# Third cross attention: GpSimd splits rows one tile at a time, and the output projection moves among the last two units

## The reference

```
xn = layer_norm(x_context, g1, b1)                  # 8 x 1601 x 256
ln_lat = layer_norm(latents, g2, b2)                # 8 x 64 x 256
q = ln_lat @ Wq                                     # 16 heads of 64
k, v = split(concatenate([xn, ln_lat]) @ Wkv)       # 1665 keys
weight = softmax(where(mask, q k^T / 8, -max))
out = (weight @ v) @ Wout                           # 1024 -> 256
x = x + out
```

## Time and profile before

| | before |
|---|---|
| median of 3 runs | 2664.39 us |
| the profiled execution, device time | 2679.92 us |
| its span | 2677.9 us |
| TensorE busy | 2377.3 us (89%) |
| VectorE busy | 1717.3 us (64%) |
| ScalarE busy | 1180.1 us (44%) |
| GpSimd busy | 892.6 us (33%) |
| mean granted TensorE clock | 0.956 |
| first and last instruction of the changed layer, about | 973 and 1679 us |

### The profile page before, as it was taken

The page is one execution under the profiler, slowest core; times in us unless marked ns, Lnnn a source line. Parts: engine busy times, 40 slices in busy tenths (PEclk is TensorE's granted clock), DMA queues, the critical chain, the costliest instruction groups (busy, mean ns, idle before and its releaser), DMA issues. The chain is left out here.

```text
span 2677.9 us, 44545 instructions
## 1 busy us (share of the span) xinstructions
PE 2377.3 (89%) x17457; PEld 1500.8 (56%) x17457; DVE 1717.3 (64%) x3309; ACT 1180.1 (44%) x1964; POOL 892.6 (33%) x543
## 2 busy tenths in 40 slices
PE   6866779999998879999999998689889999997898
PEld 4744446666663445556555565345546666665555
DVE  4986455555538586888888853754675665555577
ACT  2316134444443214555555553544445555553244
POOL 5610042224204312211222200068643454341286
PEclk8987889999998989999999999899999999999999
DMA  3200453323204025667765663033323233120132
GB/s 109 68 1 1 134 134 89 99 72 81 73 20 159 1 74 137 129 127 140 146 140 117 116 116 65 32 95 101 102 62 81 64 80 87 38 62 21 49 95 67
DMA packets 358464, 226.42 MB, mean 85 GB/s; under 512 B 289785, under 2 KB 326482, under 8 KB 358258
## 3 DMA queue, kind: packets, MB, share of 16 engines
q1 hardware_dynamic: 355186, 215.20, 33.3%
q0 software_dynamic: 3072, 8.39, 1.1%
HBM read 114.87 MB, written 0.52 MB: 43 GB/s over the span
## 5 line engine op out<-in xcount | busy, mean ns | idle before, releaser
L98 PE MATMUL PS<-hot 128*128 128x512 f16 x519 | 159.8, 451 | 97.1 <-DVE l0a_g L1053 18.3
L3891 PE MATMUL PS<-l2x_rows,l2x_pth 128*128 128x512 f16 x832 | 202.9, 383 | 17.1 <-DVE l2x_mean L4086 17.1
L3804 POOL TENSOR_TENSOR l2x_rows<-l2x_rows,l2x_one 128x1024 f16<-128x1024 f32 (+1 forms) x32 | 61.6, 1930 | 416.1 <-DVE l2x_rows L1405 416.1
L3562 DVE CUSTOM_DVE_ANT_0 l1x_junk<-PS,l1x_bias 128x1024 bf16<-128x1024 f32 (+1 forms) x128 | 123.3, 991 | 98.4 <-PE PS L3227 97.5
L4079 DVE TENSOR_TENSOR l2x_pl<-l2x_sc,l2x_ph 128x1664 f16<-128x1664 f32 x64 | 151.9, 2374 | 40.4 <-ACT l2x_ph L3960 37.8
L98 PEld LDWEIGHTS PS<-hot 128*128 128x128 f16 x519 | 53.2, 111 | 181.9 <-issue 50.7
L3562 DVE CUSTOM_DVE_ANT_0 l3x_junk<-PS,l3x_bias 128x1024 bf16<-128x1024 f32 (+1 forms) x128 | 123.6, 991 | 44.5 <-PE PS L3227 43.3
L4064 DVE CUSTOM_DVE_ANT_0 l2x_sc<-PS,l2x_bias 128x1665 f32<-128x1665 f32 x64 | 120.9, 1889 | 37.9 <-issue 37.0
L3978 ACT ACTIVATE l2x_meanT<-PS 128x256 f32<-128x256 f32 x64 | 24.5, 383 | 271.0 <-PE PS L3868 271.0
L3433 ACT ACTIVATE l3x_pT<-PS 128x512 f32<-128x512 f32 x144 | 84.6, 594 | 120.3 <-PE PS L3273 117.9
L3860 PE MATMUL PS<-l2x_kh,l2x_qth 128*128 128x512 f16 (+1 forms) x512 | 132.9, 341 | 3.8 <-DMA l2x_kl<-l2x_rows 3.8
(11 more groups left out here) (845 smaller groups left out, 6309.0 us busy)
## 6 DMA issues: line engine op xcount, KB each, us to landing
l2f_unit<-in_L_ffn_units_dram SPq DMA_DIRECT2D x36, 384.0 KB, 3.1
l3f_unit<-in_L_ffn_units_dram SPq DMA_DIRECT2D x34, 384.0 KB, 3.0
l1x_kst<-l1x_kh SPq DMA_DIRECT2D x128, 100.1 KB, 2.2
l3x_kst<-l3x_kh SPq DMA_DIRECT2D x128, 100.1 KB, 2.2
l2x_rows<-in_ctx_dram SPq DMA_DIRECT2D x8, 1536.0 KB
l1x_ctx<-in_ctx_t_dram SPq DMA_DIRECT2D x7, 1601.0 KB, 7.5
l3x_ctx<-in_ctx_t_dram SPq DMA_DIRECT2D x7, 1601.0 KB, 7.1
l1x_kst<-l1x_kl SPq DMA_DIRECT2D x64, 100.1 KB, 2.2
```

The lines of the kernel that those rows point to most:

```text
L98: self.nc.tensor.matmul(self.PS[:, bank, :], self.hot[:, 0:P], self.hot[:], start=True, stop=True)
L3562: v.tensor_tensor_reduce(junk[:, slot(it), 0:n], slot_banks(it)[:, 0:n], bias[:, 0 if normed else b % 2, at:at + n], 1.0, LOWEST, ALU.add, ...
L3804: nc.gpsimd.tensor_tensor(high, of, one[0:p, 0:n].unsqueeze(2).unsqueeze(3).to_broadcast([p, n, NC, P]), ALU.mult).then_inc(rows_high, 1)
L3891: nc.tensor.matmul(PS[:, ACC, :], pth[:, u % 2, m, :], rows2[:, b % 2, :, :, m, :], start=(m == 0), stop=False)
```

## The change

Two edits, both in `layer_2_xattn`.

1. GpSimd's `split_high` and `split_low` of batches 1 to 7 issue one operation for each row tile (128 x 256) instead of one for each part (128 x 1024 for four tiles). Only the last operation of a part raises the semaphore. Batch 0 stays as it was.
2. The output projection is cut by token tile and moved. `project_heads(t, heads)` does token tile t for a range of head pairs: tile 0 before the sums of unit 62, tile 1 before those of unit 63, tile 2 after unit 63, tile 3 with its first seven head pairs after the last mean's transposes, and its last head pair at the end. Tiles 0 and 1 go to bank 4, tile 2 to bank 6, tile 3 to bank 0. VectorE adds tiles 0 and 1 before the last mean, and tiles 2 and 3 one by one after it.

```diff
+    OUT_AT = [(PREP[0], 0), (PREP[0], D), (PREP[1], 0), (0, 0)]
...
+                def pieces(b, n):
+                    return [slice(i, i + 1) for i in range(n)] if b else [slice(0, n)]
+
                 def split_high(b, j):
                     n, p, of, high, _ = part_of(b, j)
                     pool.wait_ge(rows_made, NP_ * b + j + 1)
-                    nc.gpsimd.tensor_tensor(high, of, one[0:p, 0:n].unsqueeze(2).unsqueeze(3).to_broadcast([p, n, NC, P]), ALU.mult).then_inc(rows_high, 1)
+                    for at in pieces(b, n):
+                        i = at.stop - at.start
+                        last = nc.gpsimd.tensor_tensor(high[:, at], of[:, at],
+                                                       one[0:p, at].unsqueeze(2).unsqueeze(3).to_broadcast([p, i, NC, P]), ALU.mult)
+                    last.then_inc(rows_high, 1)
 
                 def split_low(b, j):
                     n, p, of, high, low = part_of(b, j)
                     pool.wait_ge(rows_high, NP_ * b + j + 1)
-                    nc.gpsimd.tensor_tensor(low, of, high, ALU.subtract).then_inc(rows_low, 1)
+                    for at in pieces(b, n):
+                        last = nc.gpsimd.tensor_tensor(low[:, at], of[:, at], high[:, at], ALU.subtract)
+                    last.then_inc(rows_low, 1)
...
+                def project_heads(t, heads):
+                    last_unit = (2 * t + 1) * R + heads[-1]
+                    pe.wait_ge(post_read, 2 * (last_unit + 1))
+                    bank, at = OUT_AT[t]
+                    for r in heads:
+                        last = nc.tensor.matmul(PS[:, bank, at:at + D], oT[:, r, t * P:(t + 1) * P],
+                                                wo[:, r, :], start=(r == 0), stop=(r == R - 1))
+                    if r == R - 1:
+                        last.then_inc(put_out, 1)
+
                 def unit(b, r):
                     u = b * R + r
                     if u + 2 < U:
                         scores(u + 2)
                     for group, of in fills(b, r):
                         prepare(group, of)
+                    if u == U - 2:
+                        pe.wait_ge(prep_read, len(made_as))
+                    if u + 2 >= U:
+                        project_heads(u + 2 - U, range(R))
                     pe.wait_ge(high_turned, 16 * (u + 1))
                     pe.wait_ge(sums_copied, u)
...
+                project_heads(2, range(R))
                 turn_means(U - 1)
+                pe.wait_ge(scored, U)
+                project_heads(3, range(R - 1))
                 project(U - 1)
-                pe.wait_ge(post_read, 2 * U)
-                st.end(project_tokens(k, two_banks(k, 0), [oT[:, r, :] for r in range(R)],
-                                      [wo[:, r, :] for r in range(R)]), "projected")
+                project_heads(3, range(R - 1, R))
...
+                dve.wait_ge(put_out, 2)
+                first_pair = k.X[:, 0:2, :].rearrange("p t d -> p (t d)")
+                link(v.tensor_tensor(first_pair, first_pair, PS[:, PREP[0], :], ALU.add))
                 make_means(U - 1)
-                st.wait(dve, "projected")
-                st.end(add_to_latents(k, 0), "added")
+                for t in range(2, NT):
+                    dve.wait_ge(put_out, t + 1)
+                    last = v.tensor_tensor(k.X[:, t, :], k.X[:, t, :], PS[:, OUT_AT[t][0], 0:D], ALU.add)
+                    if t == 2:
+                        link(last)
+                st.end(last, "added")
```

More of the change, by code:

```diff
@@ L3665, in ready @@
         return 1 + max(made_as[b, g] for g in groups)
-    st = Stages(k.sem("l2x_stage"), ["lat", "lat_psum", "lat_first", "lat_rest", "projected", "added"])
+    st = Stages(k.sem("l2x_stage"), ["lat", "lat_psum", "lat_first", "lat_rest", "added"])
     paced, tokens_high, tokens_low = k.sem("l2x_paced"), k.sem("l2x_tokens_high"), k.sem("l2x_tokens_low")
@@ L3680, in layer_2_xattn @@
     post_made, post_read = k.sem("l2x_post_made"), k.sem("l2x_post_read")
+    put_out = k.sem("l2x_put_out")
     with ExitStack() as c_:
```

## The result

The changed kernel takes 2639.26 us (median of four runs, 2637.24 to 2640.17), the kernel before 2662.72 us in four runs (2660.50 to 2664.89). The ratio is 0.9908, with a 95% interval of 0.989 to 0.9925: 0.9% faster.

A forecast was written before the change was run, and what follows sets the result against it. TensorE was taken to bound the kernel, idle in the layer's middle only for VectorE's mean. Splits -9.0 and tail -9.9 make -18.9 us: 2664.39 to 2645.5 us, with an 8-in-10 range of 2640 to 2660.

The forecast's parts named there:

- TensorE sets the pace: From 1040 to 1640 us TensorE bounds the layer, idle only for VectorE's mean: 14 waits, 12.2 us.
- `pl` gets in behind the first piece, at 2.3 us.: VectorE's `pl` beside GpSimd's splits: near 2.3 us in 18 places instead of 3.5 to 3.6, within TensorE's 0.57 us slack.
- The rival of four high pieces: Beside the splits, `pl` waits for all four high pieces: +7 us in the middle, 2661.5 us in all; chance 0.14.
- the one of all eight: Beside the splits, `pl` waits for all eight pieces of a part: +53 us, 2707 us in all; chance 0.06.
- The lean on L1597: VectorE gets in between queued GpSimd operations, as row L1597 did, though L123 stood 6.76 us through several.
- The first wait goes to 0, the second to 0.3, the 0.88 stays, the 0.50 is open; -9.0.: TensorE's waits for the mean in six batches: 1.15 us to 0, 0.66 to 0.3; the splits' term, -9.0 us.
- 12.2 us is all that any change of GpSimd's work can give.: Upper bound on the splits' gain in this layer: TensorE's summed idle waits for the mean, 12.2 us.
- The tail, -9.9.: Layer's end, moved output projection: 7.1 us of idle time filled and shorter addition, 2.8 us of clock; -9.9 us.
- The basis, 2664.39 us.: Starting time of the whole kernel before, the runs' median, from which the forecast's terms were subtracted.
- the pieces give back half: Low pieces hold `shift` and the scalings, so waits return next unit: splits give 2.5 us, 2652 in all; chance 0.20.
- The tail does not shrink: Layer's end: VectorE's addition delays the last mean or the clock falls; worth 3 us, inside the range, no separate chance.

The follow-up runs named there:

- e1: The kernel before with only the one-tile GpSimd splits of batches 1 to 7, old output projection; 2650.79 us, ratio 0.9957 to the kernel before.
- e7: The changed kernel with whole-part splits that, in batches 1 to 7, wait for the unit's `pl` to end; ratio 0.9905 to the kernel before.
- e9: The changed kernel with batch 0's splits also issued one tile to an operation; ratio 0.9908 to the kernel before.
- e4: The changed kernel with `split_high` issued whole again and only the low split tile by tile; ratio 0.9952 to the kernel before.
- e2: The changed kernel with the old whole-part splits, so only the moved output projection is new; 2652.41 us, ratio 0.9962 to the kernel before.
- e8: The changed kernel with batch 0's splits waiting until VectorE has written the normalised latents; ratio 0.9884 to the kernel before.

## Why the prediction was right in kind and short in size

Step by step, as it was put:

- **"TensorE sets the pace"; it stands idle "for one reason only", VectorE's mean.** Right in what counts, though the list that was read for it has a second entry, 1.2 us for ScalarE's `l2x_qb`, which no edit here touches. Taking the waits for the mean away gives the time, in e1 and e7 alike, and GpSimd's 26 us of more work (892.6 to 918.4 busy) cost nothing.
- **"`pl` gets in behind the first piece, at 2.3 us."** Right, but only at the first part of each of the six batches (2.33), six of the 18 places where 2.3 us was foretold; at the other twelve `pl` took 1.87, for the reason below. The slack of 0.57 us covered it. The rival of four high pieces and the one of all eight are refuted by that row. The lean on L1597 was right for high pieces; in e9 the low ones did what L123's row had shown. The Trainium skill's rule ("SBUF — State Buffer", section "Who interferes with whom": issue order decides who blocks) agrees with `pl` at 2.33, at 1.87 when it was issued 0.09 us ahead, and with the high pieces; by the same rule the L4161 of e9, issued 0.47 us ahead of the first low piece, would have got in behind at most the piece that ran, and it stood 8.95 us.
- **"The first wait goes to 0, the second to 0.3, the 0.88 stays, the 0.50 is open; -9.0."** This is the step that failed, by size: the mechanism held, and the term of -9.0 us measured -12.6, the shrinking of the middle. Two parts are measured. *The second wait went to 0, not 0.3* (6 x 0.3 = 1.8 us): the working had `shift` and the scaling held by the low pieces, about 1 us together and the next `pl` as late as before. `shift` was held by nothing (0.15 us), the scalings by 0.61 us, and just this hold put `pl` ahead of GpSimd (1.87 us). That a stage can be late enough to win the next one was not thought of. *A wait costs more than the idle time that the profile shows.* The idle time of TensorE in the middle fell from 13.39 to 2.34 us, by 11.05, and the middle by 12.58, over twelve waits: 0.13 us a wait beside its idle time, 1.5 us in all. e4 against the changed kernel gives the same (12.44 of time, 10.94 of idle time), and e1 against e2 (12.07 and 10.60), all at a granted clock of 1.00. The two that stayed fell by 0.15 and 0.13: 0.3 us. Sum: 9.0 + 1.8 + 1.5 + 0.3 = 12.6.
- **"12.2 us is all that any change of GpSimd's work can give."** Wrong: idle time is not all that a wait costs, and the list covers the middle alone. The low end of the range rested on it: e7 gives 13.8 in the middle (634.93 - 621.17), and e8 finds another 5.2 in the opening, which I had shown in the earlier trace rows and read only for how contention behaves, not as time to be won.
- **The tail, -9.9.** Right: -10.3. The idle waits went, the clock stayed up (4.89 against 7.80 us, 2.9 where 2.8 was expected; against e1's clock it would have been 1.7, and the tail's gain 34.84 - 25.57 = 9.3), and the last addition took 0.42 where 0.45 was taken. The one thing missed is a wait of 0.20 us ahead of unit 62's sums: the wait that the tile was to fill was 3.65 long, and a tile is 3.45 in a full queue.
- **The basis, 2664.39 us.** The four runs beside the changed kernel have a median of 2662.72, 1.7 us lower; with it, -12.6 and -10.3 give 2639.8, against 2639.26 measured. That the profiled execution was 17 us slower ahead of the layer was rightly kept out of the sum. Of the 6.2 us between 2645.5 and 2639.26 the middle has 3.6, the tail 0.4 and the basis 1.7; the rest was not traced. The number lies 0.7 us below the range, so that it lies outside at all is owed to the basis as well, which is chance; the 3.6 us are not.
- **The rival "the pieces give back half"** fell: the scalings are held by 0.61 us and TensorE does not wait for them. **"The tail does not shrink"** fell.

How a wait can cost more than its idle time is seen in the tail of after. The step from a tile of projection to the next sums takes 1615.64 - 1611.82 = 3.82 us where there is a wait of 0.20, and 1623.98 - 1620.53 = 3.45 us where there is none: 0.37 more, for 0.20 us of idle time. In a full queue the next matmul starts 0.17 us before the modelled end of the one before; after a wait this overlap is lost. The idle time in the profile begins only at that modelled end. In the middle, where scores stand ahead of the sums, the overlap is 0.14 us (1251.79 + 0.28 against 1251.93, TensorE of after), near the 0.13 us a wait:

```profile
1251.79 0.28 PE L3872 MATMUL PS<-l2x_kh,l2x_qtl 128*128 128x129 f16 x2
1251.93 1.02 PE L3918 MATMUL PS<-l2x_rows,l2x_pth 128*128 128x512 f16 x4
```

**Still open.** In e9 the low pieces shut out L4161 altogether, but in every batch from 1 on the scalings L1399, an operation of the same kind, get in between low pieces (2.27 us for four, not 1.66 + 2.7), and L123 itself got in ahead of the fourth low split. And 128x4 operations are held beside the splits (L121 1.82 us in the earlier trace rows) where the 128x1 `shift` is not (0.15 us). No run here separates the reasons.

## What to carry to other kernels

Where two engines hold each other up, ask which of them begins first, not only how long each operation is: one wait that starts the engine behind the pressed operation (e7) did, by the middle stretch, 1.2 us more than cutting its work into 126 more operations (669 against 543 on GpSimd). When the idle time of the bounding engine is added up, each stop costs its idle time and the overlap that is lost with it (0.13 us a stop here), so a sum of waits is a low estimate, not an upper bound. And a delay in one stage can put the next one in front: follow the contention through two successive parts before pricing the second.

## What was not expected of the hardware

- VectorE was let in at each of the twelve boundaries between GpSimd's one-tile multiplications (eleven of these operations took 0.53 or 0.54 us) and at none between its one-tile subtractions that followed at once (8.95 us, e9). The multiplications were beside 128x4 operations and the subtractions beside one of 128x256, so e9 alone does not say that it is the kind of GpSimd's operation that decides; L123, of 128x4, was held by subtractions too (6.76 us).
- What GpSimd loses by letting VectorE in depends on what it lets in: four high pieces with `pl` among them took 3.97 us (uncut and alone 1.90), thirteen high pieces with twelve small operations among them 7.46 us, 0.57 each, as the earlier trace rows has a piece alone at 0.61.
- An operation on 128x1 elements (`shift`, 0.15 us) ran beside a GpSimd subtraction as if alone.
- The same idle time of 3.65 us before the same matmuls cost 2.9 us of clock in one execution and 1.7 us in others (granted 0.64 over 7.80 us, 0.79 over 8.20 us).
